# Attention scores as four 32-row matmul tiles over four banks, in place of a zero-padded block diagonal of keys

## What is computed

```python
# 1. attention with a triangular solve: keys against keys, then queries against keys
s = einsum('bihd,bjhd->bhij', k, k) * scale          # "low": strictly causal softmax
L = softmax(s) * beta
u = solve_triangular(L + I, v, lower=True)
attn = softmax(einsum('bihd,bjhd->bhij', q, k) * scale, causal)     # "att"
x = x + einsum('bhij,bhjd->bihd', attn, u) @ Wo
# 2. cross attention, 4 key heads for 16 query heads, causal mask  # "x"
x = x + softmax(qg @ kg.T * scale, causal) @ v @ w_out.T
# 3. a gated feed-forward layer, the best 2 of 8 experts of width 16
x = x + ffn(layernorm(x))
```

## Time and profile before

| | |
|---|---|
| median of three runs (lowest, highest) | 1975.94 us (1975.09, 1978.83) |
| profiled execution, first to last instruction | 1984.2 us; its own time beside the span is not given |
| mean granted TensorE clock | 0.932 of full speed |
| busy: PE, PEld, DVE, ACT, POOL | 1640.0, 917.5, 1184.2, 1013.6, 807.4 us |
| first solve product of the seven turns and of the last section | 164.19, 402.61, 638.59, 874.88, 1112.94, 1355.28, 1591.35, 1819.79 us |

### The profile page before, as it was taken

One profiled execution on the slowest core, in us unless ns is written; L12 is line 12 of the kernel. 1 busy time (PEld: TensorE's weight loads), 2 busy tenths in 40 slices (PEclk: granted clock), 3 DMA queues, 4 the chain that ended last, 5 costly groups with the idle time before them and its releaser, 6 DMA issues.

```text
span 1984.2 us, 45066 instructions
## 1 busy us (share of the span) xinstructions
PE 1640.0 (83%) x14576; PEld 917.5 (46%) x14576; DVE 1184.2 (60%) x2380; ACT 1013.6 (51%) x4021; POOL 807.4 (41%) x1317
## 2 busy tenths in 40 slices
PE   5847997789977998769987799687997789977777
PEld 2424554445444554445544455354554455444434
DVE  3574567635875458644685366853577635875455
ACT  1524565456653557435574355645565455654553
POOL 1261138603385125831268112871238603384010
PEclk9968999999998999889998899988998899989889
DMA  6122011210123101130011300213012210122000
GB/s 166 40 62 66 18 35 44 61 47 17 38 49 82 29 15 40 38 91 20 17 38 38 99 17 17 49 33 88 17 38 47 57 45 17 38 49 74 10 0 22
DMA packets 213312, 87.66 MB, mean 44 GB/s; under 512 B 157000, under 2 KB 194248, under 8 KB 213072
## 3 DMA queue, kind: packets, MB, share of 16 engines
q1 hardware_dynamic: 210944, 80.90, 17.1%
q10 hardware_dynamic: 2128, 3.67, 0.6%
HBM read 42.58 MB, written 25.17 MB: 34 GB/s over the span
## 4 chain that ended last, share of the span: by engine, by line
issue 47%; POOL 29%; PE 14%; DVE 4%; ACT 2%; POOLq 1%; DMA 1%; SPq 0%; DVEq 0%; ACTq 0%
POOL blk L1134 9%; POOL outer L1132 9%; PE bank L350 4%; POOL tc L1113 3%; PE bank L281 3%; PE bank L269 2%; PE bank L300 2%; POOL prob L1120 1%; PE bank L255 1%; PE bank L338 1%; POOLq L1088 1%; POOL xr L1154 1%; ACT prob L574 1%; POOL xrs L1145 1%; DVE xt L762 1%
## 5 line engine op out<-in xcount | busy, mean ns | idle before, releaser
L574 ACT ACTIVATE prob<-bank,nmax 128x128 f32<-128x128 f32 x1536 | 543.7, 392 | 412.0 <-DVE nmax L815 343.1
L815 DVE TENSOR_REDUCE nmax<-bank 128x4 f32<-128x512 f32 x384 | 258.9, 686 | 226.8 <-PE bank L282 223.1
L574 ACT ACTIVATION_READ_ACCUMULATOR prob<-bank,nmax 128x1 f32 x1536 | 354.1, 231 | 0.0
L300 PE MATMUL bank<-ident,prob 128*128 128x128 f32 x1536 | 240.5, 298 | 123.9 <-DVE prob L852 33.6
L1132 POOL TENSOR_TENSOR outer<-blk 128x30 f32<-128x30 f32 (+14 forms) x450 | 259.8, 577 | 144.8 <-DMA blk<-blk_d 113.9
L300 PEld LDWEIGHTS bank<-ident,prob 128*128 128x128 f32 x1536 | 188.5, 152 | 211.9 <-issue 102.7
L1134 POOL TENSOR_TENSOR blk<-blk,outer 128x30 f32<-128x30 f32 (+14 forms) x450 | 270.3, 601 | 35.3
L1113 POOL TENSOR_TENSOR tc<-tc,ts 128x512 f32<-128x512 f32 x64 | 81.1, 1266 | 408.7 <-DVE ts L801 408.7
L540 ACT ACTIVATE attT<-bank 128x512 f32<-128x512 f32 x256 | 140.3, 628 | 126.9 <-PE bank L300 126.7
L852 DVE TENSOR_TENSOR prob<-prob,coef 128x512 f32<-128x512 f32 x256 | 197.1, 770 | 8.7
L583 ACT ACTIVATE blk<-bank 32x256 f32<-32x256 f32 x256 | 96.0, 375 | 137.0 <-PE bank L330 134.4
(11 more groups left out here) (134 smaller groups left out, 2616.0 us busy)
## 6 DMA issues: line engine op xcount, KB each, us to landing
kbd<-kT SPq DMA_DIRECT2D x256, 64.0 KB, 2.1
blk_d<-lowT SPq DMA_DIRECT2D x128, 64.0 KB, 2.0
blk<-blk_d SPq DMA_DIRECT2D x16, 512.0 KB, 3.3
inv_d<-blk SPq DMA_DIRECT2D x16, 512.0 KB, 2.6
lowT<-inv_d SPq DMA_DIRECT2D x64, 64.0 KB, 2.3
xs<-in_x_dram SPq DMA_DIRECT2D x16, 192.0 KB, 2.8
out_dram<-xs SPq DMA_DIRECT2D x16, 192.0 KB
xn<-in_x_dram SPq DMA_DIRECT2D x16, 128.0 KB, 3.0
```

The source lines that it names most:

```text
L300: mm = pe.transpose(ps[:, r * P:(r + 1) * P], prob[:, half(sec, kind, b), c, r, :], ident[:, :])
L574: ins = act.activation(prob[:, half(sec, kind, b), c, r, :], ring_s[i % 3][:, r * P:(r + 1) * P], ACT.Exp, bias=nmax[:, half(sec, kind, b) ...
L815: dve.tensor_reduce(nmax[:, half(sec, kind, b), c * HC:(c + 1) * HC], ring_s[i % 3][:, :].rearrange("p (h j) -> p h j", h=HC), AX.X, ALU.m ...
```

## The change

Each head's scores become a matmul tile of 32 rows (its channels) by 128 columns, read straight from `kT` and `qT` (or `kxT` and `qxT`). The heads r = 0 to 3 of a column block c use four row groups and write four different banks, so a unit of 16 heads fills four banks together; the masks are written first, for all four banks, then the tiles for c = 0 to 3. The last tile of each bank signals it. `kbd`, `kxbd`, `spread` and the DMA waits are gone. `ring_s` has four banks, `ring_a` two. The heads are stored in the order `slot(h)`. The lists of PE, ACT and DVE are written anew around whole units; the list of POOL is unchanged, and SP's only loses the `kbd` transfers.

```diff
-        ring_a, ring_d, ring_s = bank[0:3], bank[3:5], bank[5:8]
+        ring_a, ring_d, ring_s = bank[0:2], bank[2:4], bank[4:8]
...
-                def scores(stat, keys, mask, kind, b, chunks=range(NC)):
-                    for c in chunks:
-                        ps = fill("s", ring_s, exp_done, (kind, b, c))
-                        pe.matmul(ps[:, :], stat(c), keys(c), start=True, stop=False)
-                        pe.matmul(ps[:, :].rearrange("p (h j) -> p h j", h=HC), identb[:, :],
-                                  masks[:, mask, b, :].unsqueeze(1).broadcast_to([P, HC, P]),
-                                  start=False, stop=True).then_inc(s_full, 1)
+                def scores(stat, keys, mask, kind, b):
+                    tops = [fill("s", ring_s, exp_done, (kind, b, 0))]
+                    for r in range(HC):
+                        if r > 0:
+                            tops.append(fill("s", ring_s, exp_done, (kind, b, r)))
+                        pe.matmul(tops[r][:, :].rearrange("p (c j) -> p c j", c=NC), identb[:, :],
+                                  masks[:, mask, b, :].unsqueeze(1).broadcast_to([P, NC, P]), start=True, stop=False)
+                    for c in range(NC):
+                        for r in range(HC):
+                            mm = pe.matmul(tops[r][:, c * P:(c + 1) * P], stat(c, slice(Q * r, Q * r + Q)), keys(c, slice(Q * r, Q * r + Q)),
+                                           start=False, stop=(c == NC - 1))
+                            if c == NC - 1:
+                                mm.then_inc(s_full, 1)
...
-                    solve_blocks(0); query_scores(1, gs, [0]); solve_rhs(1); query_scores(1, gs, [1])
-                    solve_blocks(1); query_scores(1, gs, [2]); solve_rhs(2); query_scores(1, gs, [3]); solve_blocks(2)
+                    solve_blocks(0); query_scores(1); solve_rhs(1)
+                    solve_blocks(1)
...
-                    solve_rhs(3)
+                    solve_rhs(2)
                     project(0, "q")
-                    solve_blocks(3)
+                    solve_blocks(2); solve_rhs(3); solve_blocks(3)
                     project(0, "v"); project(0, "beta")
-                    att_mix(0); probs_T("att", 1, gs); att_out(0); query_scores(2, gs, lo)
+                    query_scores(2)
+                    att_mix(0); probs_T("att", 1, gs); att_out(0)
                     rotated_T(0)
-                    query_scores(2, gs, hi); att_mix(1)
+                    att_mix(1)
                     project(1, "k")
-                    probs_T("att", 2, gs); att_out(1); query_scores(3, gs, lo)
+                    query_scores(3)
+                    probs_T("att", 2, gs); att_out(1)
...
-                    rotated_T(1); norm_T(2)
+                    rotated_T(1); norm_T(2); key_scores(0)
                     probs_T("att", 3, gs); att_out(2)
...
-                    rotated_T(2); norm_T(3); probs_T("low", 0, gk, lo); key_scores(1, lo); probs_T("low", 0, gk, hi)
-                    project(3, "k"); key_scores(1, hi)
-                    xq_T(0)
+                    rotated_T(2); norm_T(3); probs_T("low", 0, gk)
+                    project(3, "k")
+                    xq_T(0); cross_scores(0)
                     project(3, "q")
-                    cross_scores(0, lo)
                     project(3, "v"); project(3, "beta")
-                    probs_T("low", 1, gk, lo)
-                    cross_scores(0, [2])
-                    probs_T("low", 1, gk, hi)
-                    cross_scores(0, [3])
-                    rotated_T(3); key_scores(2, lo)
+                    probs_T("low", 1, gk)
+                    rotated_T(3); key_scores(2)
                     xq_T(1)
...
+                    probs_T("x", 0, gs); cross_scores(1); cross_mix(0); cross_out(0)
+                    probs_T("low", 2, gk); key_scores(3)
+                    xq_T(2); probs_T("x", 1, gs); cross_scores(2); cross_mix(1)
+                    probs_T("low", 3, gk)
+                    cross_out(1)
+                    xq_T(3); probs_T("x", 2, gs); cross_scores(3)
+                    cross_mix(2); norm3_T(0); cross_out(2); hidden(0)
+                    query_scores(0)
+                    probs_T("x", 3, gs); cross_mix(3); norm3_T(1); norm3_T(2); cross_out(3); hidden(1); hidden(2)
...
-                    mix_out("mix", 0); att_T_out(1); exps("att", 2, lo)
+                    exps("att", 2, lo); mix_out("mix", 0); att_T_out(1); exps("att", 2, hi)
                     rotated_out(0)
-                    exps("att", 2, hi); mix_out("mix", 1); att_T_out(2); exps("att", 3)
+                    mix_out("mix", 1); exps("att", 3, lo); att_T_out(2); exps("att", 3, hi)
...
-                    att_T_out(0, "x"); exps("x", 1, [0]); mix_out("xmix", 0); exps("x", 1, range(1, NC))
+                    att_T_out(0, "x"); exps("x", 1, lo); mix_out("xmix", 0); exps("x", 1, hi)
...
+                    row_max("x", 0)
+                    beta_out(3); low_out(1)
+                    scale("x", 0, lo)
+                    row_max("low", 2)
+                    scale("x", 0, hi); row_max("x", 1)
+                    low_factors(2); scale_low(2, range(NC))
+                    cross_queries(2); add_out("xout", 0, stats3)
+                    low_out(2); row_max("low", 3)
+                    scale("x", 1); row_max("x", 2)
+                    low_factors(3); scale_low(3, range(NC))
+                    cross_queries(3)
+                    low_out(3)
+                    scale("x", 2, lo); add_out("xout", 1, stats3)
+                    scale("x", 2, hi); row_max("x", 3); norm_ffn(0)
                     scale("x", 3, lo); add_out("xout", 2, stats3); hidden_out(0); norm_ffn(1)
```

214 lines of the change are left out of this document (55 added, 159 removed).

## The result

The changed kernel takes 2168.23 us (median of four runs, 2164.27 to 2174.91) against 1975.51 for the kernel before in the same comparison: ratio 1.0975, 95% interval 1.0933 to 1.1017. The forecast was 2063 with a range of 2015 to 2110, so its direction was right, and the 87 us that it gave are less than half of the 193 that came. The profiled run took 2164.27 us with a span of 2162.5 and a mean granted clock of 0.854 (before: 0.932).

A forecast was written before the change was run, and what follows sets the result against it. A turn was taken as a loop of PE up to `low_out(1)`, POOL's inversion and rotations, then the tail. Per turn -1.5 + 4.5 + 8.5 + 1 = 12.5 us, 87 over seven turns: median 2063, range 2015 to 2110.

The forecast's parts named there:

- Unit: PE's scores of four chunks: 2.1 us instead of 4.3, 2.2 saved per unit, 12 units per turn.
- Transfers at nothing: Removing 32 `kbd` transfers per turn from SP's queue, with their waits, was costed at nothing.
- New waits up to `low_out(1)`: PE's added waits for ACT and DVE from att(2) to low(1), 18.0 us per turn against 1.85 before.
- Net +5 us: Stretch up to `low_out(1)`: waits of 18.0 against 1.85, PE saving 11, so `low_out(1)` 4.5 us later.
- The solve: Moving `project(0,"q")` ahead of `solve_blocks(2)` and shortening the scores there gains about 1.5 us per turn.
- Whatever PE saves after `low_out(1)` and before 1050 is not worth anything; whatever delays POOL costs its full length.: Between `low_out(1)` and rotation 3 POOL alone sets the pace; its 8.5 us delay counts in full each turn.
- The POOL link: Behind `low_out(1)`, POOL's inversion waits for DVE's `cross_queries(2)`: 9.5 us laid out, 8.5 taken per turn.
- The whole inversion, so the next solve: Toward the turn's end: the inversion waits for POOL, and the next solve needs its result; within the 8.5 us.
- Ring waits small: PE's small waits from two-bank `ring_a`: 0.3 at mix(1), 0.7 at kT, 0.7 at low(0), 0.2 at norm transposes.
- The tail: From rotation 3 to the next solve: two units save 4.3, waits 2.2, 1.9 and 1.3; +1 us per turn.
- First and last section: Outside the seven turns: fewer SP waits and later scores first, slower PE and ACT alternation last; 0, within 8 us.
- Rival A: PE's saving goes through: faster, up to 17 us per turn, 1860; with half of it 1918; chance 0.18.

The follow-up runs named there:

- e1: Changed kernel with one move in VectorE's list: the queries of batch row 2 ahead of the maxima of x(1); 2152.17 us, ratio 1.0895.
- e14: Changed kernel with ScalarE's copies ahead of exponentials in the att stage and batch row 2's queries ahead of the maxima of x(1); 2072.12 us, 1.0483.
- e3: Kernel before, orders and block diagonals kept, only the rings changed: `ring_a` two banks, `ring_s` four; 2029.25 us, 1.0255.
- e4: Changed kernel with the two tile loops exchanged, so tiles of one row group follow each other; 2176.17 us, 1.1008.
- e8: Kernel before, its rings and orders kept, each bank of scores made of four small tiles in turn, new head layout, no block diagonal; 2082.63 us, 1.0559.
- e2: Changed kernel with ScalarE's copies ahead of all exponentials behind the scores of att(2), att(3) and low(0); 2086.41 us, 1.0572.
- e11: Kernel before with its block diagonal, rings and products; only TensorE's single banks of scores joined into pairs; 2043.14 us, 1.0343.
- e7: Changed kernel with ten unread products ahead of the third transposes of att(1), att(2) and att(3); 2168.96 us, 1.0988.
- e13: Changed kernel with att-stage copies first, low(3) ahead of x(1) on TensorE, ScalarE and VectorE, batch row 2's queries ahead of x(1)'s maxima; 2072.48 us, 1.0487.
- e9: Kernel before, its rings and nearly its orders, no block diagonal, score banks filled in pairs so two small tiles overlap; 2065.03 us, 1.0431.
- e6: Changed kernel with each of a unit's four banks filled and released by itself: mask, its four tiles in turn, signal; 2507.65 us, 1.2725.

## Why the prediction was right and wrong

- *Unit.* Taken as 2.1 us, is 2.06, and not the 4.4 of tiles one after another. The parts are off by 0.1 each, against one another: the masks take 0.95 (forecast 0.86), the tiles 1.11 (1.25).
- *Transfers at nothing.* Right: no wait of PE in the kernel before was for a `kbd` transfer.
- *New waits up to `low_out(1)`.* 18.0 forecast, 17.0 measured: 2.59, 3.57 and 3.16 for the three units (forecast 3.0, 4.2, 3.3), 3.57 for beta (3.3), 0.95 + 0.76 for x(0) (2.0). (The terms listed for low(1) ahead of `beta_out` add to 7.9 us and not to 8.1, which changes nothing.)
- *What failed first: "Net +5 us", `low_out(1)` 4.5 later.* The sum holds every other matmul at its old length; the granted clock is a term put at nothing without a word. But behind the long stops and the solve the clock is at its lower level: `project(0,"v")` took 6.03 us, two projections 5.29, against 3.70 and 3.60 before, when the granted clock of the stage was 1.00. That is 5.7 us, and twelve transposes in 3.02 us, where a chunk of four took 0.44, add 1.7. In all, the units took 11.2 us less of TensorE in this stage, but its busy time fell only 1.9, from 92.85 to 90.97: its other products took 9.3 us more. Waits 15.2 more and busy time 1.9 less are the 13.3 us that the stage grew, where 4.5 were forecast. This is the largest miss of the turn. The solve gained 1.0 in this turn (1.5 forecast).
- *What failed second: "Whatever PE saves after `low_out(1)` and before 1050 is not worth anything; whatever delays POOL costs its full length."* The POOL link was worked out well as a wait (start of the inversion 7.0 behind L as forecast; queries at L+25.2 against L+24.7; idle 11.03 against 8.5 to 9.5), and is worth 2 us (e1, e14), so another chain was as late. From `low_out(1)` to rotation 3 this turn grew by 8.8 us, close to the 8.5 that the link was given, but that is luck: e1 takes the link away and nearly all of the loss stays. The other chain, the x units' scores, maxima, exponentials, transposes, mixes and projections, was not laid out beyond x(1). It costs 12.3 us from `low_out(1)` to the gates in the median turn, where the link and the tail were given 9.5.
- *"The whole inversion, so the next solve."* Wrong for the kernel before already: POOL ends its second inversion at 1094.44 and then stands 8.13 us for VectorE before the next section's first work, and PE enters the solve at 1112.94 without a wait for the inverses. Only ahead of the last section are they a link (2.7 us).
- *Ring waits small.* Laid out as 1.9 us in four places; e3 measures 53 us in the kernel before, 6.3 us a turn. What they are in the changed orders was not measured by itself.
- *The tail* +1, measured +3.5 in this turn (rotation 3 to solve 64.8 us against 61.3). *First and last section* 0 within 8: measured 5.0 and 7.1 longer, 12 in all.
- *Rival A* needed waits under 2.2 us per unit. e4 and e8 show both sides of it: about half of TensorE's time counts in the old orders and hardly any in the new ones.

Of the 193 us, 82 are the order of ScalarE's queue in the att stage (e2), 14 the queries on top of it (e14); what stays is 96. The smaller `ring_a` costs 53 in the kernel before (e3) and larger portions cost 65 there (e11); these two were not measured in the changed kernel, and with TensorE's saving against them they needn't add up. How they share the 96 stays open, and so does the part of the clock: e7 gave two projections a turn their full clock back and left the time as it was.

## What to carry to other kernels

Before paying for a faster product, ask in what portions it hands its result on: here four banks at once, each product quicker, moved waits of 203 us ahead of TensorE's transposes, and joining banks in pairs in TensorE's list cost 3.4% with every product as before. Lay out every chain up to the end of the turn, not only the one that ends last now; a shorter wait on the old chain (e1) or an earlier input to it (e13) is worth little when another chain is as late. Do not hold the other products at their old length when the engine will stand more: here TensorE's other products took back about 138 of the 215 us that the tiles saved. And look at the engine with the long list: moving one rotation ahead of more of the inversion's small steps on GpSimd, 0.8%, was the only gain found.

## What the runs showed of the hardware

Four 32-row tiles on four row groups and four banks run together (32 passes in 1.17 us), two row groups at a time take the same for half the work (16 passes in 1.16, e9), and one row group behind a mask takes it for a quarter (8 passes in 1.15, e6). Four row groups one after another with no mask between take 2.82 us for the 32 passes (e4). Row-group tiles one after another are no match for one 128-row product with zeros: 1.41 us for a bank with its mask against 1.07. The granted clock also fell while they ran: in e6 the tiles of the fourth bank of a unit, with TensorE never idle since the first mask, took 2.07 us where those of the first took 1.15, and the mean clock of the runs with such tiles is lower (0.932 before, 0.868 in e8, 0.852 in e9, 0.769 in e6). In e8, which keeps the orders of the kernel before, TensorE is busy 90% of the span where it was 83%, and the clock is lower all the same. In the changed kernel a standstill of 2.59 us was followed by a projection at full clock (3.60 us at 1000.17), and those of 3.57 and 3.16 us by projections partly at the lower clock (5.29 each).
